# An LSTM step with h written once and its product split into 128 and 64 weight columns

## The reference

```python
xi = xt @ U_i + b_i; xg = xt @ U_c + b_c; xo = xt @ U_o + b_o
def step(carry, xs):
    h, c = carry
    i_t = jax.nn.sigmoid(xi_t + h @ V_i)
    g_t = jnp.tanh(xg_t + h @ V_c)
    o_t = jax.nn.sigmoid(xo_t + h @ V_o)
    c_new = h * c + i_t * g_t
    h_new = o_t * jnp.tanh(c_new)
    return ((h_new, c_new), h_new)
```

## Time and profile before

| | |
|---|---|
| median of the runs (3) | 3770.19 us (3760.91 to 3777.26) |
| profiled execution | 3782.08 us, its span 3780.3 us |
| busy, share of the span | PE 75%, weight loads 60%, DVE 61%, ACT 49%, POOL 22% |
| line 1042, matmuls | 2048, mean 281 ns; idle before 615.3 us |
| line 1042, weight loads | 2048, mean 216 ns; idle before 816.3 us |
| line 1051, tanh of two gates | 1024, mean 184 ns; idle before 968.2 us |
| line 1053, output gate tanhs | 2048, mean 173 ns; idle before 37.0 us |
| line 1065, scan | 1024, mean 246 ns; idle before 553.5 us |
| line 1056, tanh of c | 1024, mean 209 ns; idle before 201.0 us |
| line 1071, h | 2048, mean 181 ns; idle before 372.6 us |
| line 1074, h * c | 1024, mean 198 ns; idle before 35.6 us |

### The profile page before, as it was taken

The page is one execution under the profiler, slowest core; times in us unless marked ns, Lnnn a source line. Parts: engine busy times, 40 slices in busy tenths (PEclk is TensorE's granted clock), DMA queues, the critical chain, the costliest instruction groups (busy, mean ns, idle before and its releaser), DMA issues. The chain is left out here.

```text
span 3780.3 us, 66516 instructions
## 1 busy us (share of the span) xinstructions
PE 2827.5 (75%) x18206; PEld 2279.5 (60%) x18206; DVE 2319.0 (61%) x9905; ACT 1836.0 (49%) x6812; POOL 813.8 (22%) x1419
## 2 busy tenths in 40 slices
PE   4777777777777777777777777777777667888666
PEld 2555555666666666666666666666656554555655
DVE  4666666666666666666666666666654431555877
ACT  1345555555555555555555555555554431443332
POOL 2332222222222222222222222222221000000010
PEclk9776766787878787877787877787876658999767
DMA  2000000000000000000000000000000001000000
GB/s 87 9 29 15 16 16 15 16 16 16 16 16 16 16 16 16 16 16 16 16 16 16 16 16 16 16 16 16 16 17 13 7 1 24 1 1 1 7 7 8
DMA packets 53965, 59.42 MB, mean 16 GB/s; under 512 B 26448, under 2 KB 45008, under 8 KB 53200
## 3 DMA queue, kind: packets, MB, share of 16 engines
q1 hardware_dynamic: 53584, 54.98, 4.7%
HBM read 42.35 MB, written 4.19 MB: 12 GB/s over the span
## 5 line engine op out<-in xcount | busy, mean ns | idle before, releaser
L1042 PE MATMUL psL<-r_h,lvab 128*96 128x16 f32 x2048 | 415.1, 281 | 615.3 <-DVE r_h L1071 573.6
L1042 PEld LDWEIGHTS psL<-r_h,lvab 128*96 128x96 f32 x2048 | 348.5, 216 | 816.3 <-DVE r_h L1071 750.3
L1051 ACT ACTIVATE r_wk<-psL 64x16 f32<-64x16 f32 x1024 | 188.4, 184 | 968.2 <-PE psL L1042 966.5
L1071 DVE SCALAR_TENSOR_TENSOR r_h<-r_wk,r_tc 64x8 f32<-64x8 f32 x2048 | 370.6, 181 | 372.6 <-ACT r_tc L1056 355.0
L1065 DVE TENSOR_TENSOR_SCAN r_c<-r_wk 64x24 f32<-64x24 f32 x1024 | 251.6, 246 | 553.5 <-ACT r_wk L1051 542.8
L1147 PE MATMUL psL<-img,dg 128*128 (+1 forms) x2744 | 459.0, 322 | 1.4 <-DVE r_h L1071 1.4
L1147 PEld LDWEIGHTS psL<-img,dg 128*128 128x128 f32 x2744 | 421.5, 231 | 13.3 <-issue 5.3
L1053 ACT ACTIVATE r_wk<-psL 32x8 f32<-32x8 f32 x2048 | 354.4, 173 | 37.0
L1056 ACT ACTIVATE r_tc<-r_c 64x8 f32<-64x8 f32 x1024 | 213.7, 209 | 201.0 <-DVE r_c L1065 186.5
L1074 DVE SCALAR_TENSOR_TENSOR r_wk<-r_h,r_c 64x8 f32<-64x8 f32 x1024 | 203.0, 198 | 35.6
L586 POOL TENSOR_TENSOR a_xw<-a_S,a_dtm 128x512 f32<-128x512 f32 x128 | 157.9, 1253 | 294.5 <-DVE a_dtm L512 294.5
(11 more groups left out here) (400 smaller groups left out, 6494.4 us busy)
## 6 DMA issues: line engine op xcount, KB each, us to landing
accb<-acc_in SPq DMA_DIRECT2D x64, 512.0 KB, 4.0
a_xy<-a_E SPq DMA_DIRECT2D x512, 16.0 KB, 1.8
W<-pack_in SPq DMA_DIRECT2D x1, 3165.0 KB, 14.3
x6d<-X SPq DMA_DIRECT2D x64, 32.0 KB
out_x<-X SPq DMA_DIRECT2D x32, 64.0 KB, 1.6
X<-x_in SPq DMA_DIRECT2D x1, 1856.0 KB, 18.2
W<-pack_in SPq DMA_DIRECT2D x1, 1331.0 KB, 5.9
X<-x_in SPq DMA_DIRECT2D x1, 192.0 KB, 7.1
```

The source lines that it names most:

```text
L1042: nc.tensor.matmul(psL[0:RM, par, c:c + 2 * LB], lvab[:], h, start=False, stop=False, skip_group_check=True).then_inc(sem("r_z"), 1)
L1051: nc.scalar.activation(o, psL[0:64, par, c:c + 2 * LB].rearrange("p (g b) -> p g b", b=LB), ACT.Tanh).then_inc(sem("r_gi"), 1)
L1071: last = v.scalar_tensor_tensor(r_h[64 * s:64 * s + 64, t + 1, s], TO, 1.0, r_tc[:], ALU.add, ALU.mult)
```

## The change

- r_h holds h once (8 columns for each step, on partitions 0 to 63; partitions 64 to 127 stay zero), and line 1071 writes it once. POOL's copy reads it there.
- The product becomes two matmuls on the same 8 columns. The first has 128 weight columns: gate g and the whole output gate, into psL's rows 0 to 127, columns of the first set. The second has 64 weight columns: gate i, into rows 0 to 63 of the second set. r_z is signalled by the second. The weights lie in lv, whose partitions 64 to 127 are zero.
- The input projections are split in the same way (128 and 64 rows instead of 96 and 96).
- The output gate has one tanh of 64 x 8 instead of two of 32 x 8.
- The scan asks for r_gi first and for r_hc second; h asks for r_tc first and, every eighth step, for r_hT second.
- The setup zeroes partitions 64 to 127 of lv and fills lua, lub and lv with two more instructions than before.

```diff
-            nc.tensor.matmul(ps[0:RM, :, 0], lua[:], xv, start=True, stop=False, skip_group_check=True)
+            nc.tensor.matmul(ps[:, :, 0], lua[:], xv, start=True, stop=False, skip_group_check=True)
             yield SLOT["r"]["xp"][1]
-            nc.tensor.matmul(ps[0:RM, :, 1], lub[:], xv, start=False, stop=False, skip_group_check=True).then_inc(sem("r_xp"), 1)
+            nc.tensor.matmul(ps[0:64, :, 1], lub[:], xv, start=False, stop=False, skip_group_check=True).then_inc(sem("r_xp"), 1)
...
-                h = r_h[:, t if t else TT].rearrange("p s b -> p (s b)")
+                h = r_h[:, t if t else TT]
                 c = t * 2 * LB
-                nc.tensor.matmul(psL[0:RM, par, c:c + 2 * LB], lvab[:], h, start=False, stop=False, skip_group_check=True).then_inc(sem("r_z"), 1)
+                nc.tensor.matmul(psL[:, par, c:c + LB], lv[:, 0:P], h, start=False, stop=False, skip_group_check=True)
+                nc.tensor.matmul(psL[0:64, par, c + LB:c + 2 * LB], lv[:, P:], h, start=False, stop=False, skip_group_check=True).then_inc(sem("r_z"), 1)
...
-                for s in range(2):
-                    nc.scalar.activation(TO[32 * s:32 * s + 32], psL[64:RM, par, c + s * LB:c + (s + 1) * LB], ACT.Tanh)
+                nc.scalar.activation(TO, psL[64:P, par, c:c + LB], ACT.Tanh)
...
+                dve.wait_ge(sem("r_gi"), n)
                 dve.wait_ge(sem("r_hc"), n)
-                dve.wait_ge(sem("r_gi"), n)
                 v.tensor_tensor_scan(r_c3[:, t % 2, :], r_wk[:, 0:24], r_wk[:, 30:54], 0.0, ALU.mult, ALU.add).then_inc(sem("r_c"), 1)
                 yield t
+                dve.wait_ge(sem("r_tc"), n)
                 if t % QT == 0:
                     dve.wait_ge(sem("r_hT"), i * 4 + (t // QT + 1))
-                dve.wait_ge(sem("r_tc"), n)
-                for s in range(2):
-                    last = v.scalar_tensor_tensor(r_h[64 * s:64 * s + 64, t + 1, s], TO, 1.0, r_tc[:], ALU.add, ALU.mult)
-                last.then_inc(sem("r_hr"), 1)
+                v.scalar_tensor_tensor(r_h[0:64, t + 1], TO, 1.0, r_tc[:], ALU.add, ALU.mult).then_inc(sem("r_hr"), 1)
                 dve.wait_ge(sem("r_hr"), n + 1)
-                v.scalar_tensor_tensor(r_wk[:, 32:56:3], r_h[0:64, t + 1, 0], 0.5, r_c3[:, t % 2, 2::3], ALU.mult, ALU.mult).then_inc(sem("r_hc"), 1)
+                v.scalar_tensor_tensor(r_wk[:, 32:56:3], r_h[0:64, t + 1], 0.5, r_c3[:, t % 2, 2::3], ALU.mult, ALU.mult).then_inc(sem("r_hc"), 1)
...
+            v.memset(lv[64:P], 0.0)
...
-                v.tensor_scalar(lub[:], w("ub"), 0.5, None, ALU.mult)
-                v.tensor_scalar(lvab[0:64, 64:RM], w("vab", 64, RM)[0:64], 0.25, None, ALU.mult)
-                v.tensor_scalar(lvab[64:P], w("vab")[64:P], 0.25, None, ALU.mult)
-                v.tensor_scalar(lvab[0:64, 0:64], w("vab", 0, 64)[0:64], 0.5, None, ALU.mult)
+                v.tensor_scalar(lua[:, RM:P], w("ub", 64, RM), 0.5, None, ALU.mult)
+                v.tensor_scalar(lub[:], w("ub", 0, 64), 0.5, None, ALU.mult)
+                v.tensor_scalar(lv[0:64, 0:64], w("vab", 0, 64)[0:64], 0.5, None, ALU.mult)
+                v.tensor_scalar(lv[0:64, P:], w("vab", 0, 64)[64:P], 0.25, None, ALU.mult)
+                v.tensor_scalar(lv[0:64, 64:RM], w("vab", 64, RM)[0:64], 0.25, None, ALU.mult)
+                v.tensor_scalar(lv[0:64, RM:P], w("vab", 64, RM)[64:P], 0.25, None, ALU.mult)
```

More of the change, by code:

```diff
@@ L173, in build @@
         bn0b = resident("bn0b", P, 2, 4)
-        lua = resident("lua", 65, RM)
-        lub = resident("lub", 65, RM)
-        lvab = resident("lvab", P, RM)
+        lua = resident("lua", 65, P)
+        lub = resident("lub", 65, 64)
+        lv = resident("lv", P, 192)
         wr8 = resident("wr8", 64, E)
@@ L253, in build @@
         r_wk = sb("r_wk", 64, 96); r_c3 = sb("r_c3", 64, 2, 24); r_tc = sb("r_tc", 64, LB)
-        r_h = sb("r_h", P, TT + 1, 2, LB)
+        r_h = sb("r_h", P, TT + 1, LB)
         r_hT = sb("r_hT", 64, B, TT)
@@ L1083, in lstm_pool @@
                 settle(pool)
-                nc.gpsimd.tensor_copy(r_hT[:, :, QT * q:QT * q + QT].rearrange("p b t -> p t b"), r_h[0:64, QT * q + 1:QT * q + QT + 1, 0])\
+                nc.gpsimd.tensor_copy(r_hT[:, :, QT * q:QT * q + QT].rearrange("p b t -> p t b"), r_h[0:64, QT * q + 1:QT * q + QT + 1])\
                     .then_inc(sem("r_hT"), 1)
```

## The result

The changed kernel takes 3824.05 us (median of 4 runs, 3818.45 to 3833.21) against 3770.81 for the kernel before beside it: a ratio of 1.0146, 95% interval 1.0121 to 1.0171. It is slower by 53 us where 140 were forecast. The profiled execution is the one of 3833.21 us.

A forecast was written before the change was run, and what follows sets the result against it. PE, ACT and DVE were all taken to bound the LSTM, in different steps. Prices of +181 and +140 us less gains of 177 gave +144, rounded to +140: 3770 + 140 = 3910 us, range 3790 to 4060.

The forecast's parts named there:

- the ring: LSTM step's loop through PE, ACT, DVE and back; longer products were to cost 517 steps x 0.35 = +181 us.
- A (no stall): Rival at the LSTM's second product: no stall where the product width changes, 3784 us; chance 0.13.
- B (the clock rises): Rival: PE's clock in the LSTM rises because PE has more to do, 3640 us; chance 0.07.
- C (all at half clock): Rival: PE's queue bounds the LSTM nearly everywhere and the clock sinks, 4055 us and above; chance 0.10.
- The second product: The added 64-column matmul in each LSTM step, behind the 128-column one: counted as 263 us of price.
- the output tanh: One output gate tanh on ACT instead of two, 0.18 us for 0.36: counted as 33 us of gain.
- the single write of h: h written once at line 1071: 0.165 us off in 639 steps where PE waits for h, 105 us gained.
- the swap: Exchanged order of waits: 0.07 us at the scan, counted as 39 us, plus 5 us at h.
- 829 steps: LSTM steps, of 1024, in which a longer product was to cost time: 517 and 312.
- PE's queue: LSTM steps where PE's own queued work, not h, is late: 312 x 0.45 = +140 us.
- surcharge: In the 312 queue steps, 0.45 us instead of 0.35, because what follows the product on PE also loads later.
- Term (3): One output gate tanh on ACT lets the tanh of c begin earlier: 0.06 us in 553 steps, 33 us.

The follow-up runs named there:

- swap_only: The kernel before with only the order of waits exchanged at the scan and at h: 3748.72 us, ratio 0.9934.
- wide_only: swap_only with lvab and lua padded by 32 zero columns, from 96 to 128, both output tanhs kept: 3803.18 us, ratio 1.0081.
- one_wide: swap_only with a single product 128 wide and one output tanh, h still written twice: 3736.73 us, ratio 0.9907.
- h_twice: The changed kernel with h also written to partitions 64 to 127 of r_h: 3955.14 us, ratio 1.0491.
- both_wide: The changed kernel with the second product padded by zero columns to 128, so no width changes: 3842.09 us, ratio 1.0178.
- narrow_first: The changed kernel with its two products exchanged, 64 wide first and 128 wide signalling z: 3884.88 us, ratio 1.0289.
- zero_upper: three_narrow with a fourth 64-column product of zeros, second in order, written to partitions 64:128: 3676.01 us, ratio 0.9742.
- zero_lower: three_narrow with a fourth 64-column product of zeros, second in order, written to partitions 0:64: 3839.45 us (median of three), ratio 1.0173.
- zero_product: The kernel before with a second product of 64 zero weight columns behind its own, which signals z: 3968.56 us, ratio 1.0515.
- three_narrow: The changed kernel with three products of 64 columns instead of 128 and 64, the output gate's with its own signal: 3653.57 us, ratio 0.9666.
- six_narrow: three_narrow with each 64-column product split into two of 32, z's four first: 3582.60 us, ratio 0.9486.
- split_wide: one_wide with its 128-column product split into four of 32 columns: 3640.08 us, ratio 0.9646.
- split_before: The kernel before with only its 96-column product split into three of 32 columns: 3724.23 us, ratio 0.9867.
- three_late: three_narrow with z signalled by the third product and no separate signal for the output gate: 3668.54 us, ratio 0.9719.

## Why the prediction was right in direction and wrong in size

**The units held.** The second load 0.07 us ahead of the first product's end, z at about 0.60 and 0.91 us, where the prediction had 0.59 and 0.95 from the first matmul's start; the scan 0.04 us behind the gate tanh; h 0.17 us shorter; a step at half clock longer by 0.10 us, for 0.15 foretold; the mean clock unchanged. The mean of z rose by 0.778 - 0.449 = 0.329 us, and 0.35 was the price in the ring. Rivals A (no stall), B (the clock rises) and C (all at half clock) are each refused by a row: the load at 0.07, the clock of 0.75, and a measured time of 3824. The time alone would have misled: it lies in the stated range, but nearer to A's 3784 than to the forecast 3910.

**What failed is the sum**: four terms were mis-sized, mainly in the number of steps in which they count. The second product was put at 263 us and cost 218, the output tanh at 33 and gave 66, the single write of h at 105 and gave 131, and the swap at 44 and gave 23. From one run to the next:

| step | counted | measured |
|---|---|---|
| waits swapped (before to swap_only) | -44 | -23 |
| 96 to 128 columns (to wide_only) | +58 | +54 |
| one output tanh (to one_wide) | -33 | -66 |
| second product (to h_twice) | +263 | +218 |
| h written once (to the changed kernel) | -105 | -131 |
| sum | +139 | +52 |

The sum is 5 us below the prediction's +144, which set the swap at h against the input projection.

- The second product, 45 us of the miss. The prediction took 829 steps, 517 of the ring and 312 of PE's queue, at 0.28 us for this product (0.35 less 0.07 for the wider first one), and a surcharge of 0.10 us (0.45 for 0.35) in the 312, because what follows the product loads late too: 232 + 31 = 263 us. Mean z rises by 0.259 us from one_wide to h_twice, and 829 x 0.259 = 215 us, near the 218 measured. So 17 us are the unit, and the total leaves no room for the 31 of the surcharge if the 829 steps are right. That it is nothing isn't shown, though: in h_twice the first load comes 0.070 us later behind h than in one_wide, and both_wide, without a change of width behind z, got some 30 us back. No run here measures by itself what a change of width behind z costs; narrow_first shows that one ahead of the first load costs 61 us more.
- The output tanh, 33 us. Term (3) counted the 0.06 us that the ring gains when the tanh of c begins earlier. Rows 2 said that in most steps the tanh of c is late by ACT's own queue, and the prediction said so too, but its sum left those steps out. By the traces it comes 0.108 us earlier in the mean of all steps (wide_only to one_wide), and the mean step gets 0.069 us shorter.
- h written once, 26 us. The sum counted 0.165 us in the 639 steps in which PE waits for h. By the traces of h_twice and the changed kernel h is 0.184 us shorter in the mean of all steps, and the first load comes 0.052 us later behind it: PE's queue takes back only that much, and 1024 x 0.132 = 135 us are left, near the 131.
- The swap, 21 us the other way. 23/0.07 = 329 steps and not 553 plus those of h; in the changed kernel only 10.5 us. A wait for the gate tanh in rows 2 doesn't say that the tanh of c follows the scan at once. From the kernel before to swap_only the scan comes 0.069 us sooner behind the gate tanh in the mean, and the tanh of c 0.039 us later behind the scan: ACT's queue takes more than half back. The 192 waits of the tanh of c for the scan, in the same rows, were the bound from below.

**Where the count ends.** The count of 829 steps, 0.81 of all, holds roughly for making the product longer. What the runs gave back per us of z over 1024 steps:

| from, to | change of mean z, us | x 1024 | measured | share | more first loads behind a change of width |
|---|---|---|---|---|---|
| zero_upper, zero_lower | +0.172 | +177 | +163 | 0.92 | |
| one_wide, h_twice | +0.259 | +265 | +218 | 0.82 | |
| swap_only, wide_only | +0.070 | +71 | +54 | 0.76 | |
| before, zero_product | +0.262 | +268 | +193 | 0.72 | |
| changed kernel, both_wide | +0.047 | +48 | +18 | 0.38 | |
| changed kernel, three_narrow | -0.284 | -290 | -170 | 0.59 | 331 |
| three_narrow, six_narrow | -0.152 | -156 | -71 | 0.46 | 33 |
| one_wide, split_wide | -0.240 | -246 | -97 | 0.39 | 310 |
| before, split_before | -0.173 | -177 | -48 | 0.27 | 247 |

A longer product is paid for to 0.72 to 0.92, but for both_wide, which also loses a change of width; a shorter one gives back less. One reason is in the last column, the steps more in which the first load of the ring starts 0.06 to 0.08 us ahead of the end of the matmul in front of it, by the traces: 108 of 1024 in the kernel before, 355 in split_before. A narrow first product puts a change of width ahead of the ring wherever a 128-wide neighbour stands there. By narrow_first against the changed kernel (470 such loads for 122, and 61 us) one is worth 61/348 = 0.175 us. Taken off, split_before gains 48 + 247 x 0.175 = 91 of 177 (0.51), split_wide 151 of 246 (0.61), three_narrow 228 of 290 (0.79), and six_narrow 77 of 156 (0.49). The expectations of split_before and split_wide left this out, and so promised too much. These 0.175 us are an estimate from one pair of runs, in which the changes behind z differ too. The trace of split_before, against that of the kernel before, shows at which engines the gain is lost: the gate tanh comes 0.031 us later behind z in the mean, the scan 0.036 later behind the gate tanh, and the first load 0.057 later behind h. That is 0.124 of the 0.173 us, 0.057 of it at PE and the rest at ACT and DVE. The share of steps at half clock also fell, from 0.50 in the changed kernel to 0.45 in three_narrow and six_narrow, and the runs don't part its effect from these.

**What was missing altogether.** The prediction read the array as one: a product has a width and the next one queues behind it. That a product of 64 columns leaves half of the columns free for another doesn't occur in its terms, and it is the larger effect: the changed kernel's own 192 columns, cut into sixths, take 241 us less than in 128 and 64, some 15 of them by the output gate's own signal (three_late). Rows 7 held the sign. Line 366, which the prediction took for one product, is two of 64 columns, to partitions 0:64 and 64:128: hence its four matmuls in 0.29 us. In the trace the second starts 0.007 us after the first.

## What to carry to other kernels

Cost a change to a ring of several engines in the unit first, and then count a term for each engine whose queue it leaves, not only where the ring waits: a removed instruction counts wherever its engine is late, a lengthened one in most steps, a shortened one only until the next engine is. A change of width of the products is dearer ahead of the first load than behind the signal, here by 61 us. Where a small product stands in a ring, try it in pieces of 32 columns on disjoint output partitions: here that took 48 us off the kernel before by itself, and 187 us together with the rest of the change and a signal of its own for the output gate.

## What the runs showed of the hardware

- Products to disjoint quarters of the columns run at once, loads and matmuls: four started within 0.04 us of each other in six_narrow, and 192 columns in six products bring z at 0.300 us where 128 and 64 need 0.603 (full clock). The Trainium skill, page "TensorE: Matmul & The Clock Gate", section "Part 3: Packing small matmuls — row/col tiling", describes this for packed tiles, and says there that matmuls start and end strictly in the order of the program. The trace differs in the starts: the third product of three_narrow begins ahead of the second in all 1024 steps. It has it end 0.10 us ahead too, but ends are modelled, so that isn't shown.
- The signal comes as by the program's order: in three_late the gate tanh, released by the third product, started 0.053 us after the second one's end, at either clock, though in the profile the third ends 0.10 to 0.20 us before.
- A load behind a change from 128 or 96 to 64 columns, or from 64 to 128, starts 0.071 to 0.073 us ahead of the end of the matmul in front of it, and 0.17 to 0.22 us ahead where the width stays (both_wide).
- A busier PE didn't come with a higher clock. In the window from 400 to 2700 us PE is busy for 1979.53 us in the changed kernel (0.86) at a clock of 0.77, and for 1855.05 us in six_narrow (0.81) at 0.79.
